# Making and storing the sum T3 one group later in a fused AdaLN and routed feed-forward kernel

## The chip, the cores and the metric

One Trainium2 chip, one core. The metric is the device time of the whole program in microseconds; the median of three runs is given for the kernel before. About 0.3% (4.3 us) is what a measurement of this kernel can tell from no change.

## The reference, cut to what matters

`x` has 2 x 2048 = 4096 tokens of 512 numbers, float32. The tokens are projected with a conditioned 512 x 512 weight; on the result a shared feed-forward (512 to 2048, relu, 2048 to 512) is computed for every token, and one of two experts (same sizes) for each token by the top gate score. Everything is added to `x`.

```python
    d = rsqrt(einsum('bi,io->bo', ys * ys, weight * weight) + EPS)
    xf = einsum('bsi,io->bso', x * ys[:, None, :], weight) * d[:, None, :]
    top1 = argmax(softmax(xf @ gate_w.T), axis=-1)
    masked = xf[None] * one_hot(top1).T[:, :, None]
    h = relu(einsum('end,edh->enh', masked, w1) + b1[:, None, :])
    routing_output = (einsum('enh,ehd->end', h, w2) + b2[:, None, :]).sum(axis=0)
    shared = relu(xf @ sw1 + sb1) @ sw2 + sb2
    return x + routing_output + shared
```

## The kernel before, in words

**Precision.** Every float32 operand is split into a high and a low float32r half; a product is three matmuls (high x high, high x low, low x high).

**Stages.** First the projection, in 32 tiles (to about 98 us). Then the "up" stage: hidden units from tokens, for the shared network and the experts (98 to 739 us). Then the shared "down" stage (739 to 1045 us) and the experts' down stage with a scatter of rows into the output, at the end of which GpSimd (POOL) gathers, adds and scatters rows one step after another, in an order written out by hand.

**The up stage.** The matrix product is done two blocks by two, with seven block products in place of eight. It has 8 blocks `s` of 1024 tokens, each in 4 groups `g`, so 32 groups `u = 4s + g`. Blocks 0 to 3 (groups 0 to 15) are the shared network, and only those make the sums T1 to T4. In a group TensorE runs seven steps c = 0 to 6, each for two halves p = 0, 1, and each half is six matmuls of 512 columns (line 1859). Fourteen halves, 84 matmuls, make a group. All groups' order is written out by hand per engine, and semaphores tie the engines:

- ScalarE (`take`, line 989) moves finished steps from PSUM to SBUF with the bias: step 0 to `vb11`, step 1 to `vb22`, step 2 to `vt1`, step 6 to `vb21`. It is strictly in order, so a take that waits holds up all later ones.
- VectorE (`add`, line 1407) adds steps 3, 4 and 5 from PSUM to `vb11`, `vb22`, `vt1`. ScalarE applies relu to `vb11` (line 1019) and `vb22` (line 1025). Then the four blocks B11, B22, B12, B21 of the hidden units are there.
- For groups 0 to 15 VectorE makes T1 = relu(B12) - B11 in `vt1` (line 1381), T2 = B22 - T1 in `vt2` (line 1389), T3 = T2 - B11 in place in `vb11` (line 1395), at the end of the group. T4 = B21 - T2, in place in `vb21` (line 1401), is made in the next group in front of the sums of steps 3 and 4.
- SyncE (SP) stores B11, B22, T1, T2, B21, T3 and T4, 512 KB each, to `hidden_scratch`, in a fixed order on one queue. It also loads raw weights (`raw_load`) and the token rows of the next block (`next_rows`).
- POOL, from group 10 on, gathers 48 tiles of projected rows by expert and stores them sorted (lines 808 and 815), on its own queue, tied to TensorE's progress.

**Buffers.** `vb11` has two buffers, used by even and odd groups. So the take of step 0 of group u+1 waits until the T3 of group u-1 has been stored (line 991, semaphore `t3_out`). `vb21`, `vb22`, `vt1` and `vt2` have one each: the take of step 6 waits for the T4 of the group before (line 1038), T4 waits for the store of B21 (line 1399), and T3 waits for the store of B11 (line 1393).

**TensorE's waits** (lines 1840 to 1853): step 1 waits for the takes of step 6 of the group before, step 2 for the takes of step 0 of its own group, step 3 for the sums of step 5 of the group before, step 4 for the takes of step 2, step 5 for those of step 1, step 6 for the sums of step 4.

**SP's order in group u, before:** T3(u-1), raw weights (groups 0 and 13 to 16), rows quarters 1 and 2 (g = 1), T4(u-1), B11(u), B22(u), rows quarter 0 (g = 0) or 3 (g = 1), T1(u), T2(u), B21(u).

In group 3 of a block (`more`) VectorE and ScalarE also build the next block's operand halves (`block_lo`, `block_hi`), between the other steps; in groups with `jobs` they split raw weights.

Of the kernel before, what the change touches and what calls it, by code (L numbers as in the profile page):

```python
# [36 lines left out]
BLOCKS = N // (2 * T)  # L37
PAIRS = HC // 2
GROUPS = PAIRS // 2
# [116 lines left out]
def build(nc, x_rows, x_cols, cond, w_cond, w_shared, w_pack, b1_pack, sb2_cols, b2_rows, gate, out):  # L156
# [8 lines left out]
    with ExitStack() as ctx:  # L165
# [6 lines left out]
        def sem(name):  # L172
            return ctx.enter_context(nc.semaphore(name))
# [116 lines left out]
        def up_bank(u, role):  # L290

            return turn[(3 * u + role) % TURN]
# [84 lines left out]
        ht_made = sem("ht_made")  # L377
# [83 lines left out]
        def inner_units(s, t, j, n):  # L461

            u = (2 * (s - BLOCKS) + t) * HC + j
            return inner_dram[u * P:(u + n) * P, :].rearrange("(a p) n -> p a n", p=P)
# [53 lines left out]
        def _(sp):  # L518
# [52 lines left out]
            def next_rows(s, q):  # L571

                sp.wait_ge(xw_lo, STEPS * (s + 1))
                if s + 1 >= BLOCKS and q == 0:
                    tiles_done = SORT.index(W * 2 * (s + 2 - BLOCKS) - 1) + 1
                    for i in range(RING):
                        sp.wait_ge(sorted_out[i], DMA * (tiles_done // RING))
                if s * GROUPS == LOOSE_UP[0] and q == 0:
                    sp.wait_ge(loose_up_done, 2)
                sp.dma_start(rows[q * B32:(q + 1) * B32, :, :], quad_rows(q, s + 1)).then_inc(rows_in, DMA)  # L580

            def keep(src, s, g, c):

                return sp.dma_start(hidden_units(s, c, 2 * g, 2), src)

            def keep_t3(u):

                s, g = divmod(u, GROUPS)
                sp.wait_ge(ht_made, 4 * u + 3)
                keep(vb11[u % 2][:], s, g, 4).then_inc(t3_out[u % 2], DMA)  # L590

            def keep_t4(u):

                s, g = divmod(u, GROUPS)
                sp.wait_ge(ht_made, 4 * u + 4)
                keep(vb21[:], s, g, 6).then_inc(t4_out, DMA)

            def hidden_load(n):
# [13 lines left out]
            def keep_inner(src, s, t, j):  # L612

                return sp.dma_start(inner_units(s, t, j, 2), src)

            for s in range(UPS):
                for g in range(GROUPS):
                    u = GROUPS * s + g
                    last = u == GU - 1
                    shared = s < BLOCKS  # L620
                    if 0 < u <= GROUPS * BLOCKS:
                        keep_t3(u - 1)
                    for n in RAW_AT_START.get(u, ()):
                        raw_load(n)
                    for n in HIDDEN_AT_START.get(u, ()):
                        hidden_load(n)
                    if s < UPS - 1:
                        if u == LOOSE_UP[0] + 1:
                            next_rows(s, 0)
                        for q in ROWS_AT_START.get(g, ()):  # L630
                            next_rows(s, q)
                    if 0 < u <= GROUPS * BLOCKS:
                        keep_t4(u - 1)
                    sp.wait_ge(b11_made, u + 1)
                    if shared:
                        keep(vb11[u % 2][:], s, g, 0).then_inc(b11_out[u % 2], DMA)
                    else:
                        keep_inner(vb11[u % 2][:], s, 0, 2 * g).then_inc(b11_out[u % 2], DMA)
                    if last:
                        raw_load(RAW_LAST + 1)  # L640
                    sp.wait_ge(b22_made, u + 1)
                    if shared:
                        keep(vb22[:], s, g, 5).then_inc(b22_out, DMA)
                    else:
                        keep_inner(vb22[:], s, 1, PAIRS + 2 * g).then_inc(b22_out, DMA)
                    if s < UPS - 1 and u != LOOSE_UP[0]:
                        for q in ROWS_LATE.get(g, ()):
                            next_rows(s, q)
                    for n in HIDDEN_LATE.get(u, ()):
                        hidden_load(n)  # L650
                    if last:
                        hidden_load(LOADS)
                        hidden_load(LOADS + 1)
                    if shared:
                        sp.wait_ge(ht_made, 4 * u + 1)
                        keep(vt1[:], s, g, 1).then_inc(t1_out, DMA)
                        sp.wait_ge(ht_made, 4 * u + 2)
                        keep(vt2[:], s, g, 2).then_inc(t2_out, DMA)
                        sp.wait_ge(up_kept, 8 * u + 8)
                        keep(vb21[:], s, g, 3).then_inc(b21_out, DMA)  # L660
                        continue
                    sp.wait_ge(b12_made, u - GROUPS * BLOCKS + 1)
                    keep_inner(vt1[:], s, 1, 2 * g).then_inc(t1_out, DMA)
                    if last:
                        hidden_load(LOADS + 2)
                    sp.wait_ge(up_kept, 8 * u + 8)
                    keep_inner(vb21[:], s, 0, PAIRS + 2 * g).then_inc(b21_out, DMA)
                    if last:
                        hidden_load(LOADS + 3)
# [521 lines left out]
        def _(dve):  # L1191
# [199 lines left out]
            def make_t3(u):  # L1391

                dve.wait_ge(b11_out[u % 2], DMA * (u // 2 + 1))
                dve.wait_ge(ht_made, 4 * u + 2)
                nc.vector.tensor_tensor(vb11[u % 2][:], vt2[:], vb11[u % 2][:], ALU.subtract).then_inc(ht_made, 1)
# [7 lines left out]
            def add(u, dst, c, kept, p):  # L1403

                dve.wait_ge(up_mm, PER_GROUP * u + 2 * c + p + 1)
                dve.wait_ge(up_kept, 8 * u + kept + p + 1)
                nc.vector.tensor_tensor(dst[:, p, :], up_bank(u, UP_BANK[c])[p][:], dst[:, p, :], ALU.add).then_inc(up_added, 1)  # L1407

            def up_group(s, g):
                u = GROUPS * s + g  # L1410
                jobs = RAW_JOBS.get(u, ())
                last = u == GU - 1
                more = g == GROUPS - 1 and s < UPS - 1

                if u == CHOOSE_GROUP:
                    softmax_start()
                if last:
                    last_group(u)
                    return
                if g == 2 and s < UPS - 1:  # L1420
                    for i in range(FLIPS):
                        flip(s + 1, i)
                if more:
                    block_lo(s + 1, 0)
                    x_sum_of(s + 1, 0)
                    x_sum_of(s + 1, 1)
                for n in jobs:
                    raw_sums(n)
                if g == 0:
                    block_lo(s, 5)  # L1430
                if u == RANK_GROUP:
                    count()
                if more:
                    block_lo(s + 1, 1)
                    x_sum_of(s + 1, 2)
                if g == 0:
                    block_lo(s, 6)
                if 0 < u <= GROUPS * BLOCKS:
                    make_t4(u - 1)
                add(u, vb11[u % 2], 3, 0, 0)  # L1440
                add(u, vb11[u % 2], 3, 0, 1)
                for n in jobs[:1]:
                    raw_lo(n)
                add(u, vb22, 4, 2, 0)
                for n in jobs[:1]:
                    raw_sums_lo(n)
                add(u, vb22, 4, 2, 1)
                if more:
                    block_lo(s + 1, 2)
                    block_lo(s + 1, 3)  # L1450
                    x_sum_of(s + 1, 3)
                add(u, vt1, 5, 4, 0)
                add(u, vt1, 5, 4, 1)
                if u == CHOOSE_GROUP:
                    choose()
                for n in jobs[1:]:
                    raw_lo(n)
                    raw_sums_lo(n)
                if more:
                    block_lo(s + 1, 4)  # L1460
                if u == 0:
                    for i in range(RING):
                        dve.wait_ge(xf_out[i], DMA * NT // RING)
                if s < BLOCKS:
                    make_t1(u)
                    make_t2(u)
                    make_t3(u)
                if u == RANK_GROUP:
                    places()

# [129 lines left out]
            for s in range(UPS):  # L1600
                for g in range(GROUPS):
                    u = GROUPS * s + g
# [437 lines left out]
```

## Time and profile before

| | |
|---|---|
| median of 3 runs | 1418.56 us (1415.41 to 1419.16) |
| profiled execution, its own time | 1417.61 us |
| its span | 1415.8 us |
| TensorE busy | 1384.6 us (98%) |
| VectorE, ScalarE, GpSimd busy | 904.4 (64%), 643.6 (45%), 282.3 us (20%) |
| mean granted TensorE clock | 0.991 |
| moved by DMA over the span | 317.65 MB, 224 GB/s |

The span runs from the first to the last instruction; the profiled execution's own time is 1.8 us longer. Matmul records overlap, so TensorE's busy share is not its share of peak. "Idle before <- X" in a row means that the engine stood idle for that long in front of the instruction and X ended the wait. "DMA share" is the mean busy share of 16 DMA engines; it can be a little above 1.

### The profile page before, as it was taken

Reading aid. Unit: us, or ns where it says so; the run is one execution under the profiler, and the core shown is the slowest. Engines: PE = TensorE matmul, PEld = TensorE weight load, DVE = VectorE, ACT = ScalarE, POOL = GpSimd, SP = SyncE. Lnnn points to the kernel's source line nnn. Section 1 sums busy time; section 2 is a strip of 40 time slices with the busy share of each in tenths; the row PEclk is TensorE's granted clock in tenths of the full one; section 3 lists DMA queues with packets and bytes.
Section 4 is the critical chain, followed back from the end, with each engine's and each line's share of the span. In section 5 each row is a group of like instructions: output and inputs, shape, how many; then the busy total and the mean of one; then the engine's idle time right before and its main releaser. Section 6 shows DMA issues by size and latency. Waiting matters only on the chain.

```text
span 1415.8 us, 17098 instructions
## 1 busy us (share of the span) xinstructions
PE 1384.6 (98%) x6086; PEld 1142.5 (81%) x6086; DVE 904.4 (64%) x1313; ACT 643.6 (45%) x929; POOL 282.3 (20%) x260
## 2 busy tenths in 40 slices
PE   9999999999799999999899999999999999999995
PEld 8888888888677888888788888888888888888884
DVE  7979967667497746675468868786866334333330
ACT  4456644445256556765566444544643221222220
POOL 0000005435343300000000000010011133166665
PEclk9999999999899999999999999999999999999998
DMA  6967485889999765633557888889897655366653
GB/s 203 300 227 230 172 258 192 254 276 312 343 351 349 268 173 193 194 134 119 184 192 276 273 270 255 289 270 301 272 276 260 195 154 164 116 160 171 159 132 59
DMA packets 223925, 317.65 MB, mean 224 GB/s; under 512 B 51440, under 2 KB 98544, under 8 KB 223824
## 3 DMA queue, kind: packets, MB, share of 16 engines
q1 hardware_dynamic: 200528, 267.06, 58.0%
q0 software_dynamic: 22016, 47.00, 12.3%
q10 hardware_dynamic: 1296, 2.49, 0.5%
q8 instruction: 49, 0.80, 0.2%
q14 instruction: 36, 0.29, 0.1%
HBM read 184.47 MB, written 140.90 MB: 230 GB/s over the span
## 4 chain that ended last, share of the span: by engine, by line
PE 54%; DMA 6%; POOL 4%; issue 3%; DVE 1%; ACT 0%; ACTq 0%; POOLq 0%; DVEq 0%
PE bank L1935 22%; PE bank L1859 19%; PE bank L1964 12%; DMA loose_rows<-x_rows,tab_in 6%; POOL loose_rows L846 2%; POOL out L832 2%; POOL xr L826 1%; PE bank L1878 1%; DMA hidden_scratch<-vb 0%; DMA loose_hidden<-hu 0%; PE bank L1981 0%; PE bank L1977 0%; DVE rows L1338 0%; DVE vb L1407 0%; ACTq L1055 0%
## 5 line engine op out<-in xcount | busy, mean ns | idle before, releaser
L1859 PE MATMUL bank<-xw,w_hi 128*128 128x512 f32 x1792 | 557.1, 392 | 13.6 <-issue 6.4
L1859 PEld LDWEIGHTS bank<-xw,w_hi 128*128 128x128 f32 x1792 | 338.1, 189 | 87.2 <-issue 8.4
L1374 DVE TENSOR_TENSOR hl<-hin,hl 128x512 fp32r<-128x512 f32 x352 | 236.9, 690 | 262.6 <-ACT hl L965 258.5
L965 ACT CAST hl<-hin 128x512 fp32r<-128x512 f32 x352 | 217.6, 624 | 385.8 <-PE bank L1964 214.2
L1859 PE MATMUL bank<-xw,w_lo 128*128 128x512 f32 x896 | 350.7, 391 | 0.0
L1964 PE MATMUL bank<-w_hi,hl 128*128 128x512 f32 x1024 | 315.5, 389 | 0.0
L1935 PE MATMUL bank<-hl,w_hi 128*128 128x512 f32 x896 | 275.9, 389 | 0.0
L1964 PEld LDWEIGHTS bank<-w_hi,hl 128*128 128x128 f32 x1024 | 192.2, 188 | 39.9
L1964 PE MATMUL bank<-w_lo,hl 128*128 128x512 f32 x512 | 199.2, 389 | 0.0
L1859 PEld LDWEIGHTS bank<-xw,w_lo 128*128 128x128 f32 x896 | 169.4, 189 | 35.8
L1935 PEld LDWEIGHTS bank<-hl,w_hi 128*128 128x128 f32 x896 | 168.2, 188 | 34.9
L989 ACT ACTIVATE vb<-bank,b 128x512 f32<-128x512 f32 x192 | 128.3, 687 | 107.3 <-PE bank L1859 76.8
L1935 PE MATMUL bank<-hl,w_lo 128*128 128x512 f32 x448 | 174.3, 389 | 0.0
L826 POOL DMA_INDIRECT xr<-x_rows,tab_in x32 | 34.0, 1062 | 569.8 <-ACT acc_hi L1143 454.1
L1964 PEld LDWEIGHTS bank<-w_lo,hl 128*128 128x128 f32 x512 | 96.1, 188 | 20.0
L1407 DVE TENSOR_TENSOR vb<-bank,vb 128x512 f32<-128x512 f32 x128 | 84.0, 686 | 40.0 <-PE bank L1859 39.9
L1343 DVE TENSOR_TENSOR xw<-rows,xw 128x1024 fp32r<-128x1024 f32 x56 | 67.7, 1222 | 53.0 <-ACT xw L919 50.6
L1935 PEld LDWEIGHTS bank<-hl,w_lo 128*128 128x128 f32 x448 | 84.1, 188 | 17.4
L832 POOL DMA_INDIRECT out<-res,tab x32 | 51.5, 1609 | 137.4 <-DVE res L1727 128.8
L808 POOL DMA_INDIRECT sorted_rows<-xf_scratch,tab_in x48 | 53.1, 1106 | 105.5 <-PE bank L1859 62.8
L919 ACT CAST xw<-rows 128x1024 fp32r<-128x1024 f32 x56 | 57.8, 1044 | 26.6 <-issue 18.2
L989 ACT ACTIVATE vt<-bank,b 128x512 f32<-128x512 f32 x64 | 43.5, 690 | 39.9 <-PE bank L1859 29.0
(184 smaller groups left out, 1200.1 us busy)
## 6 DMA issues: line engine op xcount, KB each, us to landing
hin<-hidden_scratch SPq DMA_DIRECT2D x112, 512.0 KB
hidden_scratch<-vb SPq DMA_DIRECT2D x80, 512.0 KB
hin<-expert_hidden SPq DMA_DIRECT2D x64, 512.0 KB
expert_hidden<-vb SPq DMA_DIRECT2D x48, 512.0 KB
hidden_scratch<-vt SPq DMA_DIRECT2D x32, 512.0 KB
w_new<-w_shared SPq DMA_DIRECT2D x52, 256.0 KB, 5.3
sorted_scratch<-sorted_rows POOLq DMA_DIRECT2D x48, 256.0 KB
ring<-x_cols SPq DMA_DIRECT2D x32, 256.0 KB, 5.4
```

The source lines that it names most:

```text
L808: pool.indirect_dma_start(sorted_rows[i][:], None, xf_rows, bass.IndirectOffsetOnAxis(tab_in[:, u:u + 1], 0)).then_inc(sorted_in[i], DMA)
L826: pool.indirect_dma_start(xr[u % XR][:], None, x_rows, bass.IndirectOffsetOnAxis(tab_in[:, u:u + 1], 0)).then_inc(xr_in[u % XR], DMA)
L832: pool.indirect_dma_start(out, bass.IndirectOffsetOnAxis(tab[:, u:u + 1], 0), res[u % W][:], None, bounds_check=N - 1, oob_is_err=False, c ...
L919: nc.scalar.copy(in_blocks(xw[:, c, 0, :, :]), X_OF[c]).then_inc(xw_hi, 1)
L965: nc.scalar.copy(hl[:, n % HL, 0, :], hin[:, n // 2 % LOADS, n % 2, :]).then_inc(hu_hi, 1)
L989: nc.scalar.activation(dst[:, p, :], up_bank(u, UP_BANK[c])[p][:], f, bias=b1[:, set_of(s), n:n + 1]).then_inc(up_kept, 1)
L1343: nc.vector.tensor_tensor(in_blocks(xw[:, c, 1, :, :]), X_OF[c], in_blocks(xw[:, c, 0, :, :]).bitcast(F32), ALU.subtract).then_inc(xw_lo, 1)
L1374: nc.vector.tensor_tensor(hl[:, n % HL, 1, :], hin[:, n // 2 % LOADS, n % 2, :], hl[:, n % HL, 0, :].bitcast(F32), ALU.subtract).then_inc( ...
L1407: nc.vector.tensor_tensor(dst[:, p, :], up_bank(u, UP_BANK[c])[p][:], dst[:, p, :], ALU.add).then_inc(up_added, 1)
L1859: last = nc.tensor.matmul(up_bank(u, UP_BANK[c])[p][:], w[:, DOWN_W[c], pair, part], xw[:, c, x, k, :], start=(c in FRESH and n == 1), sto ...
L1935: last = nc.tensor.matmul(bank[p][:], w[:, DOWN_W[c], i, part], hl[:, n % HL, h, :], start=(i == 0 and q == 0), stop=(i == PAIRS - 1 and q ...
L1964: last = nc.tensor.matmul(y_bank(v, m)[:], hl[:, n % HL, h, part], we_tile(w, e, j), start=(j == 0 and q == 0), stop=(j == HC - 1 and q == 2))
```

## The change

T3 of group u-1 is no longer made at the end of group u-1. It is made in group u, behind the sums of steps 3 and 4 (B11 and B22) and in front of the sums of step 5, and for the last one in group 16. Its store is issued behind that of B22(u) and in front of the late rows quarter, T1(u), T2(u) and B21(u). T4 keeps its place, so T4 is now counted before T3 in the semaphore `ht_made`.

```diff
             def keep_t3(u):
                 s, g = divmod(u, GROUPS)
+                sp.wait_ge(ht_made, 4 * u + 4)
+                keep(vb11[u % 2][:], s, g, 4).then_inc(t3_out[u % 2], DMA)
+
+            def keep_t4(u):
+
+                s, g = divmod(u, GROUPS)
                 sp.wait_ge(ht_made, 4 * u + 3)
-                keep(vb11[u % 2][:], s, g, 4).then_inc(t3_out[u % 2], DMA)
-
-            def keep_t4(u):
-
-                s, g = divmod(u, GROUPS)
-                sp.wait_ge(ht_made, 4 * u + 4)
                 keep(vb21[:], s, g, 6).then_inc(t4_out, DMA)
...
                     shared = s < BLOCKS
-                    if 0 < u <= GROUPS * BLOCKS:
-                        keep_t3(u - 1)
                     for n in RAW_AT_START.get(u, ()):
                         raw_load(n)
...
                         keep_inner(vb22[:], s, 1, PAIRS + 2 * g).then_inc(b22_out, DMA)
+                    if 0 < u <= GROUPS * BLOCKS:
+                        keep_t3(u - 1)
                     if s < UPS - 1 and u != LOOSE_UP[0]:
...
                 add(u, vb22, 4, 2, 1)
+                if 0 < u <= GROUPS * BLOCKS:
+                    make_t3(u - 1)
                 if more:
                     block_lo(s + 1, 2)
                     block_lo(s + 1, 3)
...
                 if s < BLOCKS:
                     make_t1(u)
                     make_t2(u)
-                    make_t3(u)
```

## Rows read from the trace of the kernel before

**Rows 1.** Windows: us, busy us (instructions) by engine, granted clock, DMA share, GB/s
```profile
231.70:250.80 19.10, 19.10 (x86) 15.83 (x85) 14.67 (x15) 12.25 (x15) 11.18 (x11) 1.00 0.50 178
...
365.40:384.50 19.10, 12.74 (x40) 9.82 (x39) 6.28 (x6) 4.17 (x7) 6.79 (x8) 0.73 1.09 317
384.50:403.60 19.10, 18.72 (x83) 15.03 (x82) 18.77 (x26) 10.84 (x14) 8.02 (x10) 1.00 0.99 362
403.60:422.70 19.10, 18.66 (x83) 15.14 (x82) 16.12 (x18) 10.35 (x14) 8.32 (x8) 1.00 0.98 353
```

**Rows 2.** TensorE's timeline: start us, us, matmuls merged; idle before them in brackets
```profile
364.12 0.74 PE L1859 MATMUL bank<-xw,w_hi 128*128 128x512 f32 x2 [1.78 <-DVE vb L1407]
...
377.90 1.22 PE L1859 MATMUL bank<-xw,w_hi 128*128 128x512 f32 x2 [6.36 <-issue]
...
394.26 0.74 PE L1859 MATMUL bank<-xw,w_hi 128*128 128x512 f32 x2 [0.38 <-DVE vb L1407]
...
414.11 0.73 PE L1859 MATMUL bank<-xw,w_hi 128*128 128x512 f32 x2 [0.43 <-DVE vb L1407]
...
434.69 0.70 PE L1859 MATMUL bank<-xw,w_hi 128*128 128x512 f32 x2 [1.24 <-DVE vb L1407]
```

**Rows 3.** Windows of two us behind TensorE's longest gap, columns as in rows 1
```profile
378.00:380.00 2.00, 2.00 (x5) 1.61 (x6) 1.09 (x1) 1.58 (x3) 1.60 (x3) 0.50 1.12 323
```

**Rows 4.** The chain that ended last: start us, us, what
```profile
434.69 28.95 PE bank L1859 x126
...
1204.22 21.80 PE bank L1964 x96
...
1228.94 1.58 POOL out L832
```

**Rows 5.** The stores' issues on SP: start us, us the issue took, line, tensors
```profile
120.98 0.51 SPq L584 DMA_DIRECT2D hidden_scratch<-vb  x1
...
154.19 0.36 SPq L584 DMA_DIRECT2D hidden_scratch<-vb  x1
...
344.26 0.36 SPq L584 DMA_DIRECT2D hidden_scratch<-vb  x1
...
348.75 0.58 SPq L584 DMA_DIRECT2D hidden_scratch<-vb  x1
...
362.97 5.44 SPq L584 DMA_DIRECT2D hidden_scratch<-vb  x1
...
396.80 0.36 SPq L584 DMA_DIRECT2D hidden_scratch<-vb  x1
...
400.03 0.36 SPq L584 DMA_DIRECT2D hidden_scratch<-vt  x1
...
416.48 0.36 SPq L584 DMA_DIRECT2D hidden_scratch<-vb  x1
```

**Rows 6.** Timelines of VectorE and ScalarE where a store's landing ended their wait
```profile
126.12 1.23 DVE L1401 TENSOR_TENSOR vb<-vb,vt 128x1024 f32<-128x1024 f32 x1 [1.06 <-DMA hidden_scratch<-vb]
...
361.04 1.23 DVE L1401 TENSOR_TENSOR vb<-vb,vt 128x1024 f32<-128x1024 f32 x1 [12.45 <-DMA hidden_scratch<-vb]
...
378.91 1.23 DVE L1395 TENSOR_TENSOR vb<-vt,vb 128x1024 f32<-128x1024 f32 x1 [10.40 <-DMA hidden_scratch<-vb]
...
350.51 0.69 ACT L989 ACTIVATE vb<-bank,b 128x512 f32<-128x512 f32 x1 [1.07 <-DMA hidden_scratch<-vb]
...
377.16 2.43 ACT L989 ACTIVATE vb<-bank,b 128x512 f32<-128x512 f32 x4 [11.40 <-DMA hidden_scratch<-vb]
...
403.08 1.27 ACT L989 ACTIVATE vb<-bank,b 128x512 f32<-128x512 f32 x2 [1.34 <-DMA hidden_scratch<-vb]
...
406.40 1.27 ACT L989 ACTIVATE vt<-bank,b 128x512 f32<-128x512 f32 x2 [2.05 <-DMA hidden_scratch<-vt]
```

**Rows 7.** Instructions of single lines: ns min/median/max, first and last start us
```profile
L1859 PE MATMUL bank<-xw,w_hi x1792: 387/389/795, 97.8 to 738.4; 128*128 128x512 f32 x200
...
L1395 DVE TENSOR_TENSOR vb<-vt,vb x16: 1224/1225/1228, 120.7 to 423.5; 128x1024 f32<-128x1024 f32 x16
```

More of the change, by code:

```diff
@@ L588, in keep_t3 @@
                 s, g = divmod(u, GROUPS)
-                sp.wait_ge(ht_made, 4 * u + 3)
+                sp.wait_ge(ht_made, 4 * u + 4)
                 keep(vb11[u % 2][:], s, g, 4).then_inc(t3_out[u % 2], DMA)
@@ L594, in keep_t4 @@
                 s, g = divmod(u, GROUPS)
-                sp.wait_ge(ht_made, 4 * u + 4)
+                sp.wait_ge(ht_made, 4 * u + 3)
                 keep(vb21[:], s, g, 6).then_inc(t4_out, DMA)
```

## The prediction, made before the change was run

> **What bounds the kernel now.** I began with the windows of one group's length (19.1 us) over the up stage [rows 1]. In an early window, 231.70 to 250.80, TensorE has no gap and the DMA engines are half busy (0.50). From 365 us on the DMA share is about 1, because POOL's sort now moves rows beside the stores; TensorE loses time there, and nearly nowhere else. Next I read its timeline [rows 2]: five gaps, 1.78 + 6.36 + 0.38 + 0.43 + 1.24 = 10.2 us. "Issue" stands beside the longest, but ScalarE's takes at 377.16 waited 11.40 us for a store [rows 6], and TensorE went on 0.74 us later. Two gaps also cost clock. Behind the 6.36 us one the granted clock is 0.50 [rows 3], the 1.2 GHz level. One half (six matmuls) at the pace of the chain, 28.95 us for 126 matmuls, takes 1.36 us once the last record's tail is off [rows 4]. From 377.90 to 393.88 are ten halves, 13.6 us of work in 16.0: some 2.2 us lost. Behind 1.78 us about as much is lost (four halves, 5.5 us, in 371.54 - 364.12 = 7.4); behind 1.24 us nothing.
>
> The chain then goes on along TensorE to 1226 us, and POOL's serial loop starts behind it at 1228.94 [rows 4]; it is serial and ends the span. A delay of the up stage moves the start of that loop and so the end, one for one.
>
> **The slack that T3 loses.** T3 sits in `vb11`, which the take of step 0 of group u+1 writes again. Before, T3(u-1) was issued about as group u began, 20 us ahead of that take. Now it is issued behind B22(u). TensorE needs the take at step 2 of group u+1. I count from the start of step 6 of group u: two halves of step 6, then four of steps 0 and 1, 6 x 1.363 = 8.2 us, less one take of 0.69 us [rows 6]: T3 has to land by 7.5 us behind that start. Without a stall step 6 starts 16.4 us into its group; the first group starts at 97.8 [rows 7].
>
> *Where the DMA engines are half idle:* B21 of group 0, issued at 120.98, lets T4 start at 126.12, so a store with another in front takes 5.1 us [rows 5, 6]. The latest B22 of the early groups is that of group 2, at 154.19, as raw weights are split between its sums. T3 goes 0.4 us later and lands by 159.7; step 2 of group 3 starts at 97.8 + 57.3 + 5.5 = 160.5, and T3 must be there by 159.8. It just fits, and it is the tightest. So groups 1 to 10: nothing.
>
> *Group 15:* B22(14) is issued at 396.80 [rows 5] and lands at 403.08, where the take of `vb22` starts [rows 6]. T1(14) is issued at 400.03 and lands at 406.40. T3(13) goes in between. Its distance behind B22 is at least that between T4(12) (377.16) and B11(13) (378.91), 1.75 us, and at most that up to T1, 3.3. I take 2.5: T3 lands at 405.6 and half a take makes it 406.3. Step 2 of group 15 would start at 394.26 + 8.2 = 402.4. Stall: **3.8 us** (3.1 to 4.6). Such a gap halves the clock: **+2.0** (0 to 2.3).
>
> *Weighed against a rule:* POOL's sort uses a queue of its own. The Trainium skill, page DMA: Bandwidth & Descriptors, section on queues, rings and completion order, says that each DMA engine takes turns packet by packet between the queue rows that have work. By it SP's queue gets half of the 362 GB/s of this window and 0.52 MB takes 2.9 us (an estimate from that page); the sum would be 0.4 higher than by my 2.5. The trace's 1.75 to 3.3 us enclose it.
>
> *Given back:* the gaps of 0.43 and 1.24 us, where sums of VectorE were late, lie behind this delay, and I estimate that the sums move by less than TensorE does (5.8 us), since VectorE was only packed, not held, there: **-1.7** (0 to -1.7).
>
> *Group 16:* group 15 builds the next block's halves, and ScalarE, in order, cannot begin those until its take of step 0 is over. I place B22(15), at 416.48 before [rows 5], at 0.9 us behind the start of step 6 (before: 2.4, with step 6 itself held). With the 6.3 us latency of B22(14) and 1.75 to 3.3 us for T3, it is there 9.0 to 10.5 us behind, against 7.5: **2.2 us** (1.5 to 3.0), and **+1.0** of clock (0 to 2). *Group 17:* one raw-weight job, B22 0.6 us ahead of step 6, so 7.5 to 9.0 against 7.5: **+0.7** (0 to 1.5).
>
> *Groups 11 to 14:* B22(12), issued at 344.26, lands at 350.51 [rows 5, 6]; T3(11) follows at 352.3 or later, where 350.6 is wanted. T3(11) then stands in front of T1 and B21(12) in a queue that fills from here on. B21(12), issued at 348.75, landed at 361.04, 12.3 us later. So T4(12), on VectorE behind that, comes 2 us later, and step 6 too. But the long gap swallows this: it ends when T4(12)'s store, issued at 362.97, lands at 377.16. In front of that store stand as many bytes as before: T3(12) has left, T3(11) has come. The SP issue itself took 5.44 us [rows 5], the queue was full, so a later T4 changes nothing. I take **0** (-2.6 to +2).
>
> **VectorE's own part.** Sixteen T3 of 1.225 us [rows 7] are moved and none added. In its new place T3 need not wait for B11's store (before: 10.40 us at 378.91 [rows 6]), but the transpose behind it waits for rows, so what it frees is idle time; nothing. In packed groups T1, T2 and B21 come up to 1.2 us later, and the next T4 with them: covered by TensorE's delay in groups 15 and 16; uncovered it would be 1.2. Sixteen issues of some 0.5 us change place on SP; SP waits for sums most of the time, nothing. In front of late rows, T1, T2 and B21 stands one more store, in front of raw weights, rows 1 and 2 and T4 one less; POOL's queue is not touched.
>
> **Sum:** 3.8 + 2.0 - 1.7 + 2.2 + 1.0 + 0.7 = +8.0 us. Against the profiled execution's 1417.61: 1425.6. That execution is 0.95 below the median, so **1426.5**. The forecast's own range is +2 to +15.
>
> **Rivals.**
> 1. *T4 goes free earlier, and the kernel is faster.* The place is the store of T4(12). If SP's queue was already backed up when T3(11) stood in its old place, T3(12)'s leaving counts in full: one store, 1.75 to 3.3 us, off the 6.36 us gap, and with VectorE 1.2 us ahead the gaps of 0.38, 0.43 and 1.24 close: -2.6 - 2.05 = -4.7, some 1414. It decides if T3(13) lands by 401.7, that is 4.5 us behind its issue at 397.2; loaded stores took 6.3 and 12.3. For it: the longest gap does end with T4's store. Against: the bytes in front of it stay the same. 0.12.
> 2. *Nothing measurable* (within 4.3 us). Total bytes are the same, and POOL, spared one store between 378 and 390 us, may be ahead of its tiles when B22(14) goes; then B22 lands a microsecond or two earlier and the three stalls shrink to 1 to 2 us each without clock loss: 1.5 x 2 - 1.7 + 1 = about +2, some 1421. 0.28.
> 3. *The loop feeds itself.* Every late take holds ScalarE up, hence the relu of B11 and B22, hence the next B22 and T3; stalls of 4 us with 2 of clock in groups 13, 15, 16 and 17, little given back: 3 x 6 - 1.7 + 2 = +18, some 1437. For it: ScalarE is strictly in order. Against: with TensorE stalled, the load on the DMA engines falls. 0.15.
>
> **How the numbers follow.** Forecast 0.45, rivals 0.12, 0.28, 0.15. The range 1414 to 1436 takes in rival 1 at its middle, rival 2 and the forecast; the upper tail of rival 3 is left out. Slower: forecast and rival 3, 0.60. Same: 0.28. Faster: 0.12.
>
> **What would show it.** Right: in TensorE's timeline new gaps of 2 to 4 us in front of step 2 of groups 15 and 16, ended by ScalarE's take of `vb11`, which itself waited for a store; granted clock 0.5 behind them; SP's T3 issues right behind B22's; the gap near 371 us about as it ends now. Wrong: no gap in front of step 2 of those groups, or the gap near 371 us ended before 376. If the early groups showed gaps at step 2, my margin of 0.1 us in group 3 was the mistake, and the time would be far above the range.

## The result and the profile after

| | before | after |
|---|---|---|
| median | 1418.93 us (8 runs beside those of after) | 1429.44 us (8 runs, 1426.87 to 1432.59) |
| ratio, 95% interval | | 1.0075 [1.0058, 1.0093] |
| profiled execution, its span | 1417.61, 1415.8 us | 1431.35, 1429.6 us |
| TensorE busy; mean granted clock | 1384.6 us; 0.991 | 1386.6 us; 0.990 |

The change makes the kernel slower by 10.5 us. TensorE's timeline of the kernel after, start and length in us, idle before in brackets, against [rows 2]:

```profile
333.40 0.70 PE L1860 MATMUL bank<-xw,w_hi 128*128 128x512 f32 x2 [0.64 <-ACT vb L989]
340.10 0.70 PE L1860 MATMUL bank<-xw,w_hi 128*128 128x512 f32 x2 [1.00 <-ACT vt L989]
355.61 0.73 PE L1860 MATMUL bank<-xw,w_hi 128*128 128x512 f32 x2 [1.38 <-ACT vb L989]
361.87 0.72 PE L1860 MATMUL bank<-xw,w_hi 128*128 128x512 f32 x2 [0.52 <-ACT vt L989]
367.88 0.73 PE L1860 MATMUL bank<-xw,w_hi 128*128 128x512 f32 x2 [0.26 <-DVE vb L1407]
379.23 1.22 PE L1860 MATMUL bank<-xw,w_hi 128*128 128x512 f32 x2 [5.62 <-ACT vb L989]
...
390.16 0.73 PE L1860 MATMUL bank<-xw,w_hi 128*128 128x512 f32 x2 [0.18 <-ACT vt L989]
398.33 0.73 PE L1860 MATMUL bank<-xw,w_hi 128*128 128x512 f32 x2 [2.43 <-DVE vb L1407]
408.62 0.73 PE L1860 MATMUL bank<-xw,w_hi 128*128 128x512 f32 x2 [1.76 <-ACT vb L989]
...
431.75 1.01 PE L1860 MATMUL bank<-xw,w_hi 128*128 128x512 f32 x2 [3.78 <-ACT vb L989]
454.35 0.70 PE L1860 MATMUL bank<-xw,w_hi 128*128 128x512 f32 x2 [1.65 <-ACT vb L989]
```

From 300 to 460 us, five gaps have become eleven (TensorE idle for more than 0.15 us). Those at 333.40, 355.61, 408.62, 431.75 and 454.35 stand in front of step 2 of groups 12, 13, 15, 16 and 17: the take of `vb11`. Those at 340.10, 361.87 and 390.16 stand in front of step 4, the take of `vt1`. ScalarE's timeline shows what the takes waited for, against [rows 6]:

```profile
332.57 1.27 ACT L989 ACTIVATE vb<-bank,b 128x512 f32<-128x512 f32 x2 [4.52 <-DMA hidden_scratch<-vb]
...
354.87 2.43 ACT L989 ACTIVATE vb<-bank,b 128x512 f32<-128x512 f32 x4 [5.35 <-DMA hidden_scratch<-vb]
361.13 1.27 ACT L989 ACTIVATE vt<-bank,b 128x512 f32<-128x512 f32 x2 [3.83 <-DMA hidden_scratch<-vt]
378.49 1.27 ACT L989 ACTIVATE vb<-bank,b 128x512 f32<-128x512 f32 x2 [8.98 <-DMA hidden_scratch<-vb]
...
407.88 1.27 ACT L989 ACTIVATE vb<-bank,b 128x512 f32<-128x512 f32 x2 [5.16 <-DMA hidden_scratch<-vb]
430.92 2.42 ACT L989 ACTIVATE vb<-bank,b 128x512 f32<-128x512 f32 x4 [7.66 <-DMA hidden_scratch<-vb]
453.52 2.42 ACT L989 ACTIVATE vb<-bank,b 128x512 f32<-128x512 f32 x4 [4.16 <-DMA hidden_scratch<-vb]
```

The takes at 332.57, 354.87, 407.88, 430.92 and 453.52 start as T3 lands, and TensorE goes on 0.7 to 0.8 us later. Over the whole kernel, ScalarE's list of waits has this kind, for `vb11`, `vb22` and `vb21` together, at 58.6 us in 15 waits; before it was 15.6 us in 4.

```profile
ACT vb L989 <- DMA hidden_scratch<-vb: 58.6, 15, 9.0
```

**A measure for all kernels.** TensorE's loss at a place is the start time of that half, less the start of the stage, less 1.3626 us for each half before it. It holds the idle time and the clock lost behind it. Before it is 13.0 us at step 6 of group 14, 15.7 at step 6 of group 18 and 30.6 at the last half of the up stage. After it is 17.8, 28.2 and 43.3. So (from the unrounded times) the change costs 4.7 us up to step 6 of group 14, 7.8 from there to step 6 of group 18, and nothing more (0.1) later in the stage. The stage begins 0.7 us earlier after (97.16 against 97.82), so a difference of two times on the clock of the trace is that much smaller than a difference of losses. The serial loop's first scatter moves by 12.0 us against 1228.94 [rows 4]; the chain of waits of after:

```profile
454.35 26.14 PE bank L1860 x114
...
1240.90 1.58 POOL out L832
```

The end moves by 13.8: 12.0 to that scatter and 1.8 in the loop. This is one execution, and an execution can lie up to 3.7 us off its kernel's median (that of e13 5.7), so where loss and ratio disagree below, the ratio decides.

### The profile page after: what moved, and what is told of

Same layout as the page of the kernel before. It is cut to its first block, busy times and chain, and to the rows that moved or that the text cites. A ratio compares the mean times of both kernels' runs of the same rounds, so it can differ in the third digit from the quotient of the medians.

```text
span 1429.6 us, 17098 instructions
## 1 busy us (share of the span) xinstructions
PE 1386.6 (97%) x6086; PEld 1141.3 (80%) x6086; DVE 901.8 (63%) x1313; ACT 639.2 (45%) x929; POOL 280.5 (20%) x260
## 4 chain that ended last, share of the span: by engine, by line
PE 54%; DMA 11%; POOL 4%; issue 4%; DVE 3%; ACT 1%; SPq 0%; ACTq 0%; POOLq 0%; DVEq 0%
PE bank L1936 21%; PE bank L1860 19%; PE bank L1965 12%; DMA loose_rows<-x_rows,tab_in 6%; DMA hidden_scratch<-vb 2%; POOL loose_rows L846 2%; POOL out L832 2%; DMA rows<-sorted_scratch 1%; DVE vb L1407 1%; DMA loose_rows<-loose_rows,loose_at 1%; POOL xr L826 1%; PE bank L1879 1%; DMA hidden_scratch<-vt 0%; ACT xw L919 0%; DMA loose_hidden<-hu 0%
## 5 line engine op out<-in xcount | busy, mean ns | idle before, releaser
L989 ACT ACTIVATE vb<-bank,b 128x512 f32<-128x512 f32 x192 | 126.2, 687 | 121.5 <-DMA hidden_scratch<-vb 58.6
L826 POOL DMA_INDIRECT xr<-x_rows,tab_in x32 | 33.4, 1044 | 580.9 <-ACT acc_hi L1143 464.5
L919 ACT CAST xw<-rows 128x1024 fp32r<-128x1024 f32 x56 | 57.8, 1045 | 27.3 <-issue 13.7
```

What stands on the lines that cost most here:

```text
L826: pool.indirect_dma_start(xr[u % XR][:], None, x_rows, bass.IndirectOffsetOnAxis(tab_in[:, u:u + 1], 0)).then_inc(xr_in[u % XR], DMA)
L919: nc.scalar.copy(in_blocks(xw[:, c, 0, :, :]), X_OF[c]).then_inc(xw_hi, 1)
L989: nc.scalar.activation(dst[:, p, :], up_bank(u, UP_BANK[c])[p][:], f, bias=b1[:, set_of(s), n:n + 1]).then_inc(up_kept, 1)
```

## The experiments

Each kernel was timed beside the kernel before, in five rounds. Differences between two ratios are good to about 0.2 points. "Loss" is the measure above, in the profiled execution, at step 6 of group 14 / at step 6 of group 18 / at the stage's last half.

| run | T3 made | its 512 KB stored | take of `vb11` waits for it | ratio, 95% | loss, us |
|---|---|---|---|---|---|
| before | own group | first in next group | yes | 1 | 13.0 / 15.7 / 30.6 |
| after | behind the sums | behind B22 | yes | 1.0075 [1.0058, 1.0093] | 17.8 / 28.2 / 43.3 |
| e1 | behind the sums | behind B22 | no | 1.0046 [1.0034, 1.0058] | 17.2 / 24.6 / 39.4 |
| e2 | own group | behind B22 | yes | 1.0044 [1.0029, 1.0058] | 12.6 / 24.3 / 40.4 |
| e3 | behind T4, ahead of the sums | behind T4 | yes | 1.0052 [1.0036, 1.0067] | 19.7 / 25.1 / 39.9 |
| e5 | own group | behind T4 | yes | 1.0001 [0.9987, 1.0015] | 14.0 / 18.4 / 33.2 |
| e8 | behind the sums | first in next group | no | 1.0011 [0.9996, 1.0027] | 14.2 / 17.6 / 33.4 |
| e9 | own group | behind B22 | no | 1.0034 [1.0019, 1.0048] | 18.1 / 23.6 / 38.0 |
| e7 | as after, T3(0) to T3(9) only | | | 1.0028 [1.0010, 1.0045] | 13.3 / 17.0 / 33.1 |
| e13 | as after, T3(10) to T3(15) only | | | 1.0054 [1.0035, 1.0074] | 19.0 / 31.0 / 47.0 |
| e10 | before, T4's store ahead of rows 1, 2 | | | 0.9996 [0.9982, 1.0011] | 13.0 / 16.3 / 31.4 |
| e14 | before, rows quarter 0 behind B21 | | | 1.0002 [0.9988, 1.0016] | 15.9 / 18.8 / 33.6 |
| e11 | before, slower sort | | | 0.9999 [0.9984, 1.0014] | 13.9 / 15.6 / 31.2 |
| e12 | after, slower sort | | | 1.0062 [1.0042, 1.0083] | 18.4 / 27.3 / 43.1 |

**e1: the gate taken off.** The kernel after, with these edits (the take of `vb22` waits for the transfer instead):

```diff
-                keep(vb11[u % 2][:], s, g, 4).then_inc(t3_out[u % 2], DMA)
+                keep(vb22[:], s, g, 4).then_inc(t3_out[u % 2], DMA)
...
-                wait(act, t3_out[u % 2], DMA * (min(u, GROUPS * BLOCKS) // 2))
+                wait(act, ht_made, 4 * min(u - 1, GROUPS * BLOCKS))
                 wait(act, b11_out[u % 2], DMA * (u // 2))
                 wait(act, b22_out, DMA * u)
+                wait(act, t3_out[u % 2], DMA * (min(u, GROUPS * BLOCKS) // 2))
```

> The changed kernel, but the late store of 512 KB reads vb22 in place of vb11 (the stored T3 is wrong; VectorE still makes it). So the same bytes stand at the same place of SP's queue, but ScalarE's take of vb11 no longer waits for them; its take of vb22, which TensorE needs three steps later, does. Theory (the late store holds the buffer that step 2 needs): the gaps of 0.6 to 3.8 us in front of step 2 of groups 12, 13, 15, 16 and 17 go, and the ratio to before is 0.997 to 1.002 (1415 to 1422 us). Rival (one more store in front of T1, T2 and B21, which land later and so delay T4 and the sums): the gaps move to step 6 and the ratio stays at 1.005 to 1.009.

Measured: 1.0046, between the two ranges. Taking the gate off gives 0.29 points back of 0.75, and leaves more than half. The gaps in front of step 2, 9.2 us in the kernel after, are gone. Up to 460 us those at step 4 have grown from 1.7 to 8.1 us in sum and those at step 6 from 2.7 to 4.7, and the long one has shrunk from 5.62 to 1.36. So the length of the gaps that a wait ends is no measure of what that wait costs. Three of them:

```profile
361.41 1.22 PE L1861 MATMUL bank<-xw,w_hi 128*128 128x512 f32 x2 [3.31 <-ACT vt L989]
376.65 0.73 PE L1861 MATMUL bank<-xw,w_hi 128*128 128x512 f32 x2 [1.36 <-ACT vb L989]
388.92 1.22 PE L1861 MATMUL bank<-xw,w_hi 128*128 128x512 f32 x2 [3.81 <-ACT vt L989]
```

**e2: made early, stored late.** The kernel before, with the store alone moved:

```diff
-                    if 0 < u <= GROUPS * BLOCKS:
-                        keep_t3(u - 1)
                     for n in RAW_AT_START.get(u, ()):
...
                         keep_inner(vb22[:], s, 1, PAIRS + 2 * g).then_inc(b22_out, DMA)
+                    if 0 < u <= GROUPS * BLOCKS:
+                        keep_t3(u - 1)
```

> The kernel before with T3 made at the end of its group as before, and only its store moved behind B22 of the next group. Theory (the landing of the store is what counts): as slow as the whole change, ratio 1.005 to 1.010, gaps in front of step 2 of groups 13, 15, 16, 17. Rival (VectorE's T3 between the sums is what makes T1, T2 and B21 late): ratio within 1.000 to 1.003.

Measured: 1.0044, again between the two ranges, with gaps of 0.15 to 3.34 us in front of step 2 of groups 12 to 17. The store's move by itself makes 0.44 of the 0.75. The other 0.31 comes only when VectorE makes T3 late as well.

**e3 and e5: behind T4.** e3 makes and stores T3 directly behind T4, ahead of the sums; e5 is the kernel before with only the store moved there, which is behind rows 1 and 2, raw weights and T4, and still in front of B11 and B22:

```diff
                         keep_t4(u - 1)
+                        keep_t3(u - 1)
                     sp.wait_ge(b11_made, u + 1)
...
                     make_t4(u - 1)
+                    make_t3(u - 1)
                 add(u, vb11[u % 2], 3, 0, 0)
...
                     make_t2(u)
-                    make_t3(u)
```

(The store's old place goes in both. e5 has the first of these three alone.)

> T3 made in the next group directly behind T4, in front of the sums, and stored directly behind T4. T4 is ahead of T3 on VectorE and on the queue, as in the change, but T3's store is issued 4 to 8 us earlier than in the change. Theory (lateness of T3 costs, T4's lead gives little because the bytes in front of its store stay the same): ratio 0.997 to 1.003. Rival (T4's lead is worth a store, 2 to 3 us, and VectorE's 1.2 us close the small gaps): ratio 0.995 to 0.997, about 1413. If even this lateness costs, ratio above 1.003, with gaps at step 2 of groups 16 and 17 where T4 comes latest.

> Only the store of T3 moved, to directly behind T4's; T3 made at the end of its group as before. It tells the queue's part of the run beside it from VectorE's part. Theory: within 0.3% of before, 0.998 to 1.003. Rival (T4's lead on the queue is worth 2 to 3 us of the longest gap): 0.996 to 0.998.

Measured: 1.0052 and 1.0001. The two have the same order of stores, so the difference, 0.51 points, is VectorE's: 1.2 us in front of every sum, plus a store of T3 that can leave only as T3 is made, 1.2 us behind T4. e3 shows it from group 2 on, in a gap of 0.81 us in front of step 6. T3 ran before in time that VectorE spent waiting for B21's store (12.45 us at 361.04 [rows 6]). And e5 says that a store may wait past T4 at no cost in sum; what costs in e2 is that it is put behind B22, where in groups 12 to 15 T1's store follows by 3 to 6 us and B21's by 5 to 9.

**e8 and e9: one part each.** In both the take of `vb11` waits only for T3 to be made. e8 makes T3 late but sends 512 KB of `vt2` at the old place of the queue. e9 makes it early and sends 512 KB of `vb22` at the new place. A buffer is still held in each: in e8 VectorE's next T2 waits until `vt2` is sent, and in e9 (as in e1) the take of `vb22` waits for the late transfer. From e8, against the kernel after:

```diff
-                sp.wait_ge(ht_made, 4 * u + 4)
-                keep(vb11[u % 2][:], s, g, 4).then_inc(t3_out[u % 2], DMA)
+                sp.wait_ge(ht_made, 4 * u + 2)
+                keep(vt2[:], s, g, 4).then_inc(t3_out[u % 2], DMA)
...
+                    if 0 < u <= GROUPS * BLOCKS:
+                        keep_t3(u - 1)
                     for n in RAW_AT_START.get(u, ()):
```

> VectorE's place of T3 alone: T3 made late, behind the sums of B11 and B22, but the 512 KB go out at their old place of SP's queue, read from vt2 (the stored T3 is wrong), and no take of vb11 waits for them. The first four runs left 0.46% that the buffer's wait does not explain. If VectorE's late T3 is the cause of it (it ran in idle time in front of T4, and now delays the sum of step 5, T1, T2 and B21's store): ratio 1.003 to 1.005, gaps in front of step 6 of groups 14 to 16, none at steps 2 and 4. If the queue's order is the cause instead: within 0.999 to 1.001.

> The queue's order alone: T3 made at the end of its group as before, its 512 KB issued behind B22 of the next group and in front of T1, but read from vb22, so that no take of vb11 waits for their landing (the stored T3 is wrong). If one more store in front of T1 is a cost (take of vt1 late, step 4 waits): ratio 1.002 to 1.004 with gaps in front of step 4 of groups 13 and 14. If VectorE's place is the whole rest: 0.999 to 1.001.

Measured: 1.0011, not clear of no change, and 1.0034, clear of it. The place in the queue, with `vb11` free and no VectorE work moved, makes nearly half of the loss. Its gaps in groups 12 to 14 stand at step 1 (the long one), step 4 (338.75, 390.07) and step 6 (the longest 366.86, 399.14), and not at step 2:

```profile
338.75 0.70 PE L1860 MATMUL bank<-xw,w_hi 128*128 128x512 f32 x2 [1.05 <-ACT vt L989]
...
366.86 0.73 PE L1860 MATMUL bank<-xw,w_hi 128*128 128x512 f32 x2 [2.42 <-DVE vb L1408]
379.33 1.22 PE L1860 MATMUL bank<-xw,w_hi 128*128 128x512 f32 x2 [6.73 <-ACT vb L989]
390.07 0.72 PE L1860 MATMUL bank<-xw,w_hi 128*128 128x512 f32 x2 [0.62 <-ACT vt L989]
399.14 0.74 PE L1860 MATMUL bank<-xw,w_hi 128*128 128x512 f32 x2 [3.32 <-DVE vb L1408]
```

The hold on `vb22` isn't what TensorE waits for. Three takes of `vb22` up to 460 us start as the late transfer lands (354.57, 383.89, 450.19), but each is over before T1's store lands and starts the take of `vt1`, and step 5, which needs `vb22`, has no gap. ScalarE's timeline of e9, with the landings of the late transfer at 354.50 and of T1 at 357.94:

```profile
354.57 1.27 ACT L989 ACTIVATE vb<-bank,b 128x512 f32<-128x512 f32 x2 [3.28 <-DMA hidden_scratch<-vb]
357.96 1.27 ACT L989 ACTIVATE vt<-bank,b 128x512 f32<-128x512 f32 x2 [2.12 <-DMA hidden_scratch<-vt]
```

**e7 and e13: which groups.** The change under a condition on u, for the first ten T3 and for the last six, in each of its places:

```diff
+                if 0 < u <= 10:
+                    make_t3(u - 1)
...
-                    make_t3(u)
+                    if u >= 10:
+                        make_t3(u)
```

> The change made for the T3 of groups 0 to 9 alone, where the DMA engines are half idle; groups 10 to 15 as before. Both theories: at most one small gap (0.6 us, group 3, a raw-weight split that comes later), ratio 0.999 to 1.002. If the change costs in every group, 1.004 or more.

> The change made for the T3 of groups 10 to 15 alone, the complement of the run with groups 0 to 9. If all of the cost lies where the DMA engines are full: ratio 1.006 to 1.009, as the whole change. If the 0.28% of the run with groups 0 to 9 are real and add up: 1.004 to 1.006.

Measured: 1.0028 and 1.0054, which together make 0.82, about as much as the change. e7 is a miss. Its trace shows one new gap among the early groups, 0.44 us at 156.90, and a loss 1.3 us above before at step 6 of group 18 and 2.5 us above it at the stage's end. The ratio says 4.0 us (1.4 to 6.4). The 1.2 us that come late in the stage may have nothing to do with the change: in groups 28 to 31 nine of the fourteen executions lose 14.7 to 15.2 us and five 16.0 to 16.5, e8 and e2 among the five, after and before among the nine. Behind the up stage, where all kernels are the same, the executions differ by 6 us (674.3 to 680.4). So one trace can't place the rest.

**e10 and e14: the order mended elsewhere.** Two tries at the kernel before. e10 puts T4's store ahead of rows quarters 1 and 2; e14 takes rows quarter 0 from in front of T1, T2 and B21:

```diff
                         for q in ROWS_LATE.get(g, ()):
-                            next_rows(s, q)
+                            if q or not shared:
+                                next_rows(s, q)
...
                         keep(vb21[:], s, g, 3).then_inc(b21_out, DMA)
+                        if g == 0 and s < UPS - 1 and u != LOOSE_UP[0]:
+                            next_rows(s, 0)
                         continue
```

> The kernel before, T3 untouched, with T4's store issued in front of rows quarters 1 and 2 in place of behind them (1 MB in front of it less, where g = 1). It tests what bounded the longest gap, 6.4 us in group 14, which ended with the landing of T4(12)'s store. If it is the bytes in front of that store: it lands 4 to 8 us earlier, the gap goes, ratio 0.994 to 0.998, given back in part where the rows come later to the transposes. Rival (the DMA engines are full, what is gained there is lost at the next landing): 0.999 to 1.001.

> The kernel before, with the late rows quarter 0 of groups 0, 4, 8 and 12 (512 KB of loads) issued behind the store of B21 instead of between the stores of B22 and T1. It is the lesson of the queue order turned round: one transfer less in front of T1, T2 and B21, whose landings set the take of vt1 (step 4) and T4 (hence the sums of step 4, and step 6). Theory 1 (any 512 KB in front of these stores sets the time, and taking one away gives some of it back): B21(12) lands 2 to 3 us earlier and the gap near 364 us (1.78 us with as much of clock) shrinks or goes; the loss summed up at step 6 of group 14 falls from 13.0 to 9 to 11 us; ratio to the kernel before 0.997 to 0.999. Theory 2 (with the DMA engines full, a gap taken away in one place comes back in another, as when T4's store was put in front of the rows): the loss by group 18 stays within 1 us of 15.7; ratio 0.999 to 1.001. Theory 3 (the rows are now late for the transposes of the next block, which stand in order on their engine): ratio above 1.002.

Measured: 0.9996 and 1.0002, nothing. In both a gap moves. e10's longest gap is about as long as before's 6.36 but in front of step 4, on T1's store; e14's gap near 364 is gone, and the next is twice as long. From the timelines of TensorE, e10 and then e14:

```profile
385.50 1.22 PE L1859 MATMUL bank<-xw,w_hi 128*128 128x512 f32 x2 [6.74 <-ACT vt L989]
```

```profile
343.97 0.70 PE L1862 MATMUL bank<-xw,w_hi 128*128 128x512 f32 x2 [0.83 <-DVE vb L1410]
...
380.75 1.22 PE L1862 MATMUL bank<-xw,w_hi 128*128 128x512 f32 x2 [12.05 <-ACT vb L992]
```

VectorE's timeline of e14 shows T4(12) at 359.70, only 1.3 us ahead of before's 361.04 [rows 6], and ScalarE's shows its store landing at 380.01, 2.9 us behind before's 377.16:

```profile
359.70 1.23 DVE L1404 TENSOR_TENSOR vb<-vb,vt 128x1024 f32<-128x1024 f32 x1 [8.87 <-DMA hidden_scratch<-vb]
```

```profile
380.01 2.42 ACT L992 ACTIVATE vb<-bank,b 128x512 f32<-128x512 f32 x4 [15.59 <-DMA hidden_scratch<-vb]
```

T4(12) was made earlier, but SP issued its store 2.9 us later than before (365.89 against 362.97); the rows that no longer stand in front of T1 and B21 still stand in front of it. Theory 2 holds by the ratio; the loss at step 6 of group 18 came out 3.1 us above before's, where it said within 1. No version here beats the kernel before.

**e11 and e12: meant as a lighter load.** Tile k of the sort is tied to TensorE's progress by 5k/2 halves in place of 2k, on before and on after:

```diff
-                pool.wait_ge(up_mm, PER_GROUP * SORT_GROUP + 2 * k)
+                pool.wait_ge(up_mm, PER_GROUP * SORT_GROUP + 5 * k // 2)
```

> The kernel before with POOL's sort spread out: tile k starts after 2.5 k halves of TensorE's work in place of 2 k, so the 48 tiles end near group 18.5 in place of 17. The same bytes, a fifth less per microsecond beside groups 12 to 16. It tests whether the full DMA engines, not the order of the stores, are the root of the 13 to 15 us that TensorE loses in groups 13 to 16. If so: ratio 0.994 to 0.998, the longest gap shorter by 2 us or more. Rival (the order and the buffers set it): 0.999 to 1.001, or above 1 if the rows of a later block now come too late.

> The changed kernel with the same slower sort. If the change costs because its store stands in front of T1, T2 and B21 in a full queue: with lighter load it costs less, ratio to the kernel before 1.000 to 1.004. If the cost lies in the semaphores and VectorE's place whatever the load: 0.75% above the run beside it, so 1.002 to 1.007 where that one gains, and no smaller distance to it.

Measured: 0.9999 and 1.0062. The load did not fall. Windows of e11, columns as in rows 1; the kernel before has 1.05 and 1.10 as DMA share there:

```profile
346.00:365.00 19.00, 18.00 (x79) 14.38 (x78) 6.87 (x9) 6.46 (x9) 6.21 (x8) 1.00 1.08 359
365.00:384.00 19.00, 10.08 (x36) 7.85 (x35) 4.67 (x5) 4.04 (x7) 6.39 (x8) 0.73 1.08 318
```

The tie isn't what holds POOL. By TensorE's times tile 18 could be gathered from 337.7 us before and from 350.1 in e11; it is gathered at 366.50 and 366.42, and the last tile at 486 and 489. The pair therefore says nothing on how the loss depends on the load. That dependence was not shown in another way.

## Why the prediction was right, and where its working was not

The side held, and so did the places: T3's landing gates the take of `vb11`, TensorE stalls at step 2 of groups 15 to 17, and the delay of the up stage (12.6 us) reaches POOL's loop (12.0, which is 12.6 less the 0.7 us by which the stage began earlier, but for rounding). 1429.4 lies in the range, 2.9 above the forecast. But the nearness is in good part luck. My sum puts the whole loss on that gate. With the gate off, e1 still loses 0.46% where the change loses 0.75; the queue's order alone makes 0.34 (e9) and VectorE's new place up to 0.31, both terms that I had at nothing. The sum was +8.0, and this execution shows +13.8, 12.6 of it in the up stage, split in another way.

**The step that failed: "Groups 11 to 14 ... I take 0".** The measure says +4.7 by step 6 of group 14. At the end of the long gap it is +2.0 (of which 0.9 lies before group 11, see below): there my working was right that a small delay comes in front, that the gap swallows some (6.36 has become 5.62), and its upper end was +2. I stopped at the gap, because "as many bytes as before" stand in front of T4(12)'s store. Behind it they don't. T3(12), long gone by then before, now stands directly in front of rows quarter 3, T1, T2 and B21 of group 13. VectorE's timelines from 375 us of before and from 380 us of after show what follows:

```profile
382.36 4.62 DVE L1338 STREAM_TRANSPOSE rows<-rows 128x1024 f32<-128x1024 f32 x4 [2.23 <-DMA rows<-sorted_scratch]
...
390.06 1.22 DVE L1401 TENSOR_TENSOR vb<-vb,vt 128x1024 f32<-128x1024 f32 x1
391.19 1.28 DVE L1407 TENSOR_TENSOR vb<-bank,vb 128x512 f32<-128x512 f32 x2
```

```profile
386.44 4.62 DVE L1338 STREAM_TRANSPOSE rows<-rows 128x1024 f32<-128x1024 f32 x4 [13.04 <-DMA rows<-sorted_scratch]
...
394.13 1.22 DVE L1401 TENSOR_TENSOR vb<-vb,vt 128x1024 f32<-128x1024 f32 x1
395.26 1.28 DVE L1407 TENSOR_TENSOR vb<-bank,vb 128x512 f32<-128x512 f32 x2
```

The rows' landing starts the transposes, and from there VectorE is packed up to the sums in both: 8.8 us to the first of them. All of it is 4.1 us later (4.7 from the stage's start); TensorE got there 2.0 later already, and the gap in front of step 6 grows by the rest, 0.38 to 2.43. I had written of the freed wait for B11 that "the transpose behind it waits for rows, so what it frees is idle time", and so saw the row that sets this time, but did not ask what a store in front of those rows does to them. e9, in which of all this only the queue's order changes, costs 0.34.

The loss at step 6 of group 14 goes with this landing in every run: where the transposes start by 382.7 us (before, e2, e5, e7, e10) it is 12.6 to 14.0 us, at 383.4 (e8, e11) 13.9 to 14.2, at 385.1 (e14) 15.9, and from 386.2 to 388.3 (e1, after, e9, e12, e3, e13) 17.2 to 19.7. But T3(12) in front of the rows doesn't make them late by itself. In e2 and e5 it stands there too, and VectorE's timelines of the two have

```profile
382.09 4.63 DVE L1338 STREAM_TRANSPOSE rows<-rows 128x1024 f32<-128x1024 f32 x4 [4.22 <-DMA rows<-sorted_scratch]
```

```profile
382.59 4.62 DVE L1337 STREAM_TRANSPOSE rows<-rows 128x1024 f32<-128x1024 f32 x4 [3.54 <-DMA rows<-sorted_scratch]
```

There T4(12)'s store had landed at 373.6 and 373.5, 5 us ahead of after's 378.5, and the rows took as long behind it as after or longer. Why T4(12) was so much earlier in these two and not in e9 (378.6) is open; e2 loses its time from step 6 of group 14 on instead.

**Group 15.** Predicted 3.8 and 2.0 of clock; measured 1.9 in all. T3(13) landed at 407.9, not 405.6, but step 2 would itself have come at 398.33 + 8.2 = 406.5 and not at 402.4: the failed step had delayed TensorE by more than the store. The clock stayed at 1.00 in the window.

**Given back, 1.7.** Right: before's gaps of 0.43 and 1.24 us, at step 6 of groups 15 and 16, have no counterpart.

**Group 16.** Predicted 2.2 and 1.0; measured 3.9 and 1.7. ScalarE's packed stretch made B22(15) late as I had it, and its store took 8.0 us to land, not 6.3. **Group 17.** Predicted 0.7, measured 1.8; another 0.6 comes at step 6 of group 18, where I looked for nothing.

```profile
403.60:422.70 19.10, 17.34 (x77) 14.04 (x76) 15.26 (x16) 11.25 (x15) 10.03 (x10) 1.00 1.01 350
422.70:441.80 19.10, 15.32 (x61) 12.22 (x60) 14.53 (x21) 8.09 (x12) 7.53 (x8) 0.91 1.00 350
```

(Windows of after, columns as in rows 1: group 15 without, group 16 with a loss of clock.)

**The distance of T3 behind B22.** I took 2.5 (1.75 to 3.3). In group 14 B22 lands at 406.23 and T3(13) at 407.86, 1.6 apart; in groups 11, 12, 13, 15 and 16 it is 1.3, 1.5, 0.8, 1.2 and 2.5. The rule of the Trainium skill (page DMA: Bandwidth & Descriptors, section on queues, rings and completion order), taken as an even half for each queue, gave 2.9 by my reading, and the trace does not agree with that half: from 405 to 409 us SP's queue moved 0.91 MB and POOL's 0.52. The section says only that an engine takes turns, a packet at a time, between queues that have work; the half was my reading.

**Groups 1 to 10: "nothing".** The tight one, T3(1) into group 3, fits: issued at 154.4, landed at 158.3, needed by 159.8. A gap of 0.45 us came there all the same, on raw weights that VectorE split 0.9 us later than before (155.11 against 154.18), as T3 now goes in front of them. (e8 has T3 in the same place and no gap: there VectorE came 0.9 us earlier into this group's work.)

```profile
156.38 0.73 PE L1860 MATMUL bank<-xw,w_hi 128*128 128x512 f32 x2 [0.45 <-DVE w_lo L1322]
```

The trace has 0.9 us for these groups, and e7 puts 0.28% on them (0.10 to 0.45), so by the ratio the term was too small by at least 1.4 us.

**VectorE's own part: "nothing".** Right in its reason and not in its size. In its new place T3 never waits, as its group among those of the instructions shows (idle before: 0.0; [rows 6] had 10.40):

```profile
L1395 DVE TENSOR_TENSOR vb<-vt,vb 128x1024 f32<-128x1024 f32 x16 | 19.4, 1214 | 0.0
```

But it stands in busy time now and stood in idle time before. With the store late too that costs 0.31 points (after less e2); with the store on time 0.11 (e8), which may be nothing. I had it "covered by TensorE's delay"; it is not.

**The rivals.** Rival 1 fell: T3(13) landed at 407.9 where it had to land by 401.7, and 5.62 is all that the long gap shrank to. Rival 2 fell too: 10.5 us (8.2 to 13.2) is more than its 4.3, and its argument that total bytes are the same is refuted by e9, where another order of the same bytes costs 0.34%. Rival 3 had one thing right, stalls in groups 12 to 17 one after another, though of 0.6 to 3.8 us and mostly without clock. (Its sum of +18 counts three stalls of 6 us for the four groups that it names; with four it would be +24.)

**What is shown and what is open.** Shown: the queue's order alone (e9 against before: 0.34, with the hold on `vb22` ruled out by its trace and not by a run); that the cost lies in its place behind B11 and B22 and not in its passing T4 (e5: 0.01); VectorE's place ahead of the sums (e3 less e5: 0.51). Barely clear of zero: the gate (after less e1: 0.29, but e2 less e9: 0.10 with 0.2 either way) and VectorE's place behind the sums (0.31). These parts overlap and don't add up to 0.75 exactly. Open: e7's cost beyond its visible gap, why T4(12)'s store is early in e2 and e5, and how the loss would fall with a lighter queue.

## What to carry to other kernels

In one queue that is full, count for each transfer not only the bytes in front of it but who waits for those behind it: putting one store of 512 KB directly in front of three whose landings are waited for cost 0.34% here without moving any other work, and putting it two places earlier, behind T4, cost nothing. A swap that only exchanges who waits behind whom (e10, e14) moved a gap here and didn't gain. And gaps that one wait ends (9.2 us at step 2) are not what you get back when you remove that wait (4 us, e1): later waits took the rest. Work put in place of a wait was free, and the same work a microsecond ahead of a sum that TensorE waits for was not (e3 less e5); when an estimate stops at "a long gap swallows it", follow the engines once more on the other side of the gap.

## What was not expected of the hardware

- Clock lost behind a gap doesn't follow its length: before, 1.78 us of idle at 364.12 was followed by about as much lost; after, 2.43 us at 398.33 and 1.76 us at 408.62 lost none (granted clock 1.00 from 398.33 to 408.33 and from 408.62 to 422.70), and 3.78 us at 431.75 lost 1.7. What the engine had done just before differs between them; no run here isolates that.
- Where the DMA share is above 1, SP can be held in the issue itself. Around the long gap (1.09 from 361.3 to 373.0) the issue of a load of rows took 5.15 us and that of the next four stores 6.44 together, where single ones elsewhere take 0.36. SP's timeline of after:

```profile
361.32 5.15 SPq L580 DMA_DIRECT2D rows<-sorted_scratch  x1
366.53 6.44 SPq L584 DMA_DIRECT2D hidden_scratch<-vb  x4
```

- A store's time from issue to landing runs from 2.8 us (T4(11) of after, 343.9 to 346.7) to 11.9 (T4(12), 366.5 to 378.5), and to 15.6 for one from `vt1` (T1(13), 373.8 to 389.4): the medians per kind of transfer (4.2 us from a `vb`, 5.2 from a `vt`) don't price one at a given place.
